# A decoder kernel: expert results added in the next block, an attention bias built later, a wait of the sorted experts moved back

## The reference, cut to what matters

```python
    # L2 ffn, second half: one of 8 experts per row
    idx = jnp.argmax(logits, axis=-1)
    mid = jax.nn.relu(jnp.einsum('th,ehf->etf', hn2, w1) + b1[:, None, :])
    y = jnp.einsum('etf,efh->eth', mid, w2) + b2[:, None, :]
    moe = y[idx, jnp.arange(hn2.shape[0])]
    ...
    x = x + _L3_attn_ref(_layernorm(x, axis=-1), ...)    # gated attention in groups of 64 rows
    x = x + _L3_xattn_ref(_layernorm(x, axis=-1), ctx_1024, ctx_1024, fside_BxS2_0, ...)
    x = x + _L3_ffn_ref(_layernorm(x, axis=-1), ...)     # two of 8 experts per row
    ...
    # in _L3_xattn_ref: the bias that is added to the scores
    ct = jnp.cumsum(session_deltas, axis=1)
    pairwise_delta = jnp.abs(ct[:, :, None] - ct[:, None, :])
    scores = scores + (time_bias_weight * jnp.log1p(pairwise_delta))[:, None, :, :]
```

## Time and profile before

| what | us |
|---|---|
| runs | 2972.42, 2975.32, 2977.95; median 2975.32 |
| the profiled execution | 2969.33 |
| its span in the trace | 2967.4 |

### The profile page before, as it was taken

One profiled execution on the slowest core, in us unless ns is written; L12 is line 12 of the kernel. 1 busy time (PEld: TensorE's weight loads), 2 busy tenths in 40 slices (PEclk: granted clock), 3 DMA queues, 4 the chain that ended last, 5 costly groups with the idle time before them and its releaser, 6 DMA issues. The chain is left out here.

```text
span 2967.4 us, 47859 instructions
## 1 busy us (share of the span) xinstructions
PE 2559.4 (86%) x16117; PEld 1874.6 (63%) x16117; DVE 1810.5 (61%) x4091; ACT 1313.7 (44%) x3205; POOL 808.7 (27%) x627
## 2 busy tenths in 40 slices
PE   4998989999688785999998989959969687869997
PEld 2666756666455453777676767649945465448886
DVE  7866976589788544344455559953355688444443
ACT  2334654266778234434343436623332565323332
POOL 5533520054000332222221216621110243132222
PEclk8999999999888798999999999979989898989999
DMA  9001000000200423000001010051120300531110
GB/s 321 2 1 49 14 19 1 15 1 1 65 4 1 109 87 125 29 1 1 1 1 50 12 42 31 2 206 37 37 76 1 90 12 1 182 118 49 51 49 26
DMA packets 152050, 142.43 MB, mean 48 GB/s; under 512 B 59948, under 2 KB 136770, under 8 KB 151428
## 3 DMA queue, kind: packets, MB, share of 16 engines
q1 hardware_dynamic: 139668, 110.61, 12.6%
q0 software_dynamic: 10560, 27.19, 2.7%
q10 hardware_dynamic: 1584, 1.57, 0.2%
HBM read 98.14 MB, written 43.02 MB: 48 GB/s over the span
## 5 line engine op out<-in xcount | busy, mean ns | idle before, releaser
L953 POOL TENSOR_TENSOR room<-room 128x1024 f32<-128x1024 f32 x144 | 273.1, 1896 | 464.0 <-DVE room L888 463.7
L882 DVE TENSOR_REDUCE room<-room 128x8 f32<-128x1024 f32 x144 | 174.1, 1209 | 0.0
L1420 PE MATMUL l3f_out<-room,Y 128*128 x624 | 141.0, 379 | 0.0
L953 POOL TENSOR_TENSOR room<-room,Y 128x1024 f32<-128x1024 f32 x32 | 60.7, 1896 | 252.0 <-DVE Y L888 252.0
L1420 PEld LDWEIGHTS l3f_out<-room,Y 128*128 128x128 f32 x624 | 115.6, 190 | 14.2
L1025 ACT ACTIVATE room<-l2a_scores,Y 128x128 f32<-128x128 f32 x256 | 71.9, 380 | 86.7 <-DVE Y L874 86.7
L609 PE MATMUL l2a_proj<-room 128*128 128x256 f32 x384 | 97.5, 398 | 11.6 <-ACT room L977 11.6
L2461 POOL DMA_INDIRECT sorted_rows<-room,l1f_place_i x32 | 31.0, 968 | 267.1 <-DVE l1f_place_i L2172 257.7
L1025 ACT ACTIVATE room<-l3x_scores,room 128x128 f32<-128x128 f32 x256 | 73.3, 401 | 55.3 <-DVE room L874 55.3
L1025 ACT ACTIVATE room<-l1a_scores,room 128x128 f32<-128x128 f32 x256 | 71.4, 386 | 58.6 <-DVE room L874 58.6
L1025 ACT ACTIVATE room<-l0x_scores,room 128x128 f32<-128x128 f32 x256 | 70.5, 384 | 59.4 <-DVE room L874 59.4
(11 more groups left out here) (838 smaller groups left out, 6909.3 us busy)
## 6 DMA issues: line engine op xcount, KB each, us to landing
sorted_rows<-head SPq DMA_DIRECT2D x1, 16640.0 KB, 57.0
room<-in_L_ffn_w SPq DMA_DIRECT2D x16, 1024.0 KB, 13.0
room<-in_L_ffn_W SPq DMA_DIRECT2D x16, 1024.0 KB, 12.0
Y<-sorted_rows SPq DMA_DIRECT2D x62, 130.0 KB, 2.1
room<-in_ctx SPq DMA_DIRECT2D x24, 256.0 KB, 2.9
room<-sorted_rows SPq DMA_DIRECT2D x39, 130.0 KB, 2.1
room<-results SPq DMA_DIRECT2D x8, 512.0 KB, 7.1
room<-in_L_ffn_routed_w SPq DMA_DIRECT2D x4, 512.0 KB
```

The lines of the kernel that those rows point to most:

```text
L882: dve.tensor_reduce(rsum[:, u % 2, :], p[:, u % (TURN + 1), :, :], AX.X, ALU.add)
L953: pool.tensor_tensor(p[:, u % (TURN + 1), :, :], p[:, u % (TURN + 1), :, :], rinv[:, u % (TURN + 1), :].unsqueeze(2).to_broadcast([P, HEAD ...
L1420: mm = pe.matmul(obank[n % 2][:, 0:D], hT[:, n % 2, f, :], chip.room[:, bass.ds(at + (SLOT // 2 + f * D), D)], start=(f == 0), stop=(f == ...
```

## The change

Three edits stand in the diff.

1. `l2fm` ends with the first group: SP fetches one piece, VectorE adds it and makes its statistics. The gated attention fetches the other three pieces into `pend` at its start. VectorE's `combine(g)` adds one group and makes its four statistics, one group in each of slots -2, -1 and 0; in slot 0 follow the roots of the 12 tiles and the second group's normalisation, which stood in slot -2.
2. `l3x`: the running-sum matmul and its copies move behind the opening's projections; the weighting is done for four tiles ahead of the slots and for the other twelve in slots 1 to 3.
3. `l3f`: `dest` gets four columns, and `aim(n)` waits for the scatter of tile n-4 instead of n-2.

```diff
@@ attention_block, tensor
-                if plan.mask == "timebias":
-                    pe.wait_ge(raw_loaded[0], 32)
-                    pe.matmul(out[:, 0:NB], chip.upper[:, :], deltas[:, :], start=True, stop=True).then_inc(ct_ready, 1)
...
-                for f in opening + bias_turns:
+                for f in opening:
+                    project((0, f))
+                if plan.mask == "timebias":
+                    pe.wait_ge(raw_loaded[0], 32)
+                    pe.matmul(out[:, 0:NB], chip.upper[:, :], deltas[:, :], start=True, stop=True).then_inc(ct_ready, 1)
+                for f in bias_turns:
                     project((0, f))
@@ attention_block, vector (the copies move likewise, behind the opening)
+                def biased(n):
+                    dve.wait_ge(log_ready, n + 1)
+                    dve.scalar_tensor_tensor(out=bias[:, n * 4:n * 4 + 4, :], in0=gap[:, n * 4:n * 4 + 4, :], scalar=w.v["tb"],
+                                             in1=keywide[:, n * TG:(n + 1) * TG].rearrange("p (j k) -> p j k", j=4), op0=ALU.mult, op1=ALU.add)
+                    dve.drain()
+
                 if plan.mask == "timebias":
                     dve.wait_ge(key_ready, 1)
-                    for n in range(NB // 4):
...
+                    biased(0)
...
+                    if plan.mask == "timebias" and 1 <= t < NB // 4:
+                        biased(t)
@@ sorted_experts_block
+    DESTS = 4 if last else 2
...
-                    for g in range(NG):
-                        for c in range(keep):
-                            part = results[c * TOK:(c + 1) * TOK, :].rearrange("(s b) d -> s b d", b=NB)[:, g * GR:(g + 1) * GR, :]
-                            sp.dma_start(back[c][:, g * GR:(g + 1) * GR, :], part).then_inc(gathered[g], 16)
+                    part = results[0:TOK, :].rearrange("(s b) d -> s b d", b=NB)[:, 0:GR, :]
+                    sp.dma_start(chip.Y[:, 0:GR, :], part).then_inc(gathered, 16)
                     prefetch.load(sp)
...
-                    if n >= 2:
+                    if last and n >= 4:
+                        dve.wait_ge(returned[par], (n // 2 - 1) * 16)
+                    if not last and n >= 2:
                         dve.wait_ge(returned[par], n // 2 * 16)
@@ gau_block, sync
+                for g in range(1, NG):
+                    part = chip.results[0:NB * P, :].rearrange("(s b) d -> s b d", b=NB)[:, g * GR:(g + 1) * GR, :]
+                    sp.dma_start(pend[:, (g - 1) * GR:g * GR, :], part).then_inc(pend_loaded[g], 16)
                 if prefetch:
                     prefetch.load(sp)
@@ gau_block, vector
+                def combine(g):
+                    dve.wait_ge(pend_loaded[g], 16)
+                    those = slice(g * GR, (g + 1) * GR)
+                    dve.tensor_tensor(chip.X[:, those, :], chip.X[:, those, :], pend[:, (g - 1) * GR:g * GR, :], ALU.add)
+                    for b in range(g * GR, (g + 1) * GR):
+                        sums(b)
...
-                        if g + 1 < NG:
+                        if 0 < g < NG - 1:
                             normalise(g + 1)
+                    if k < 1:
+                        combine(k + 3)
+                    if k == 0:
+                        dve.drain()
+                        ln_stats_vector(chip, dve, chip.X, rest, have="mv", part=slice(GR, NB))
+                        normalise(1)
@@ gau_block, scalar
+                    if k == 0:
+                        ln_stats_scalar(chip, act, rest, part=slice(GR, NB))
+                        act.preload_act_table(ACT.Silu)
```

More of the change, by code:

```diff
@@ L852, in _ @@
                         empty((0, f))
+                if plan.mask == "timebias":
+                    dve.wait_ge(raw_loaded[0], 32)
+                    for n in range(NB // 4):
+                        dve.tensor_copy(dwide[:, n * 4:n * 4 + 4, :], deltas[:, n * 4:n * 4 + 4].unsqueeze(2).to_broadcast([P, 4, P])).then_inc(wide_ready, 1)
+                    dve.wait_ge(ct_ready, 1)
+                    dve.tensor_copy(ctcol[:, :], out[:, 0:NB])
+                    dve.drain()
                 if chip.has_head:
@@ L1200, in sorted_experts_block @@
         final_rows = chip.out.rearrange("b s d -> (b s) d")
-        back = [chip.Y, chip.room[:, 0:NB * D].rearrange("p (b d) -> p b d", b=NB)]
         first_turned = 1 if chip.has_head else 0
@@ L1236, in sorted_experts_block @@
         returned = [sem("returned0"), sem("returned1")]
-        gathered = [sem(f"gathered{g}") for g in range(NG)]
+        gathered = sem("gathered")
         combined, summed = sem("combined"), sem("summed")
@@ L1734, in _ @@
                     empty_out(n)
[L1736 to L1748, removed]
+                if not last:
+                    dve.wait_ge(gathered, 16)
+                    dve.tensor_tensor(chip.X[:, 0:GR, :], chip.X[:, 0:GR, :], chip.Y[:, 0:GR, :], ALU.add).then_inc(combined, 1)
                     dve.drain()
-                    for b in range(g * GR, g * GR + 2):
+                    for b in range(2):
                         dve.bn_stats(chip.bn[:, b, :], chip.X[:, b, :])
                     dve.drain()
-                    for b in range(g * GR, g * GR + 2):
+                    for b in range(2):
                         dve.bn_aggr(chip.mv[:, b, :], chip.bn[:, b, :])
+                    dve.wait_ge(summed, 1)
+                    dve.tensor_scalar(chip.mv[:, 2:GR, 1], chip.mv[:, 2:GR, 1], 1.0 / D, None, ALU.mult)
+                    dve.drain()
+                    ln_stats_vector(chip, dve, chip.X, final, have="mv", part=slice(0, GR))
                 dve.drain()
[L1756 to L1760, removed]
-                    ln_stats_vector(chip, dve, chip.X, final, have="mv")
             @block.scalar
@@ L1822, in _ @@
                     act.preload_act_table(ACT.Sqrt)
[L1823 to L1832 removed]
+                    act.wait_ge(combined, 1)
+                    for b in range(2, GR):
+                        act.activation(chip.Y[:, b, :], chip.X[:, b, :], ACT.Identity, scale=1.0 / D, accum_out=chip.mv[:, b, 0:1])
+                    act.drain()
+                    for b in range(2, GR):
+                        op = act.activation(chip.Y[:, b, :], chip.X[:, b, :], ACT.Square, bias=chip.mv[:, b, 0:1], scale=-1.0, accum_out=chip.mv[:, b, 1:2])
+                    op.then_inc(summed, 1)
+                    ln_stats_scalar(chip, act, final, part=slice(0, GR))
             @block.gpsimd
@@ L2563, in gau_block @@
         oT = sb("oT", [P, OC, P])
+        pend = sb("pend", [P, NB - GR, D])
+        pend_loaded = [sem(f"pend{g}_loaded") for g in range(NG)]
+        rest = {n: sem(f"rest_{n}") for n in ("var_ready", "std_ready")}
         bank = [chip.ps(f"gau_bank{i}", scope) for i in range(8)]
```

24 lines of the change are left out of this document (5 added, 19 removed).

## The result

The changed kernel takes 2964.26 us in the median of ten runs (2959.86 to 2969.99), the kernel before 2980.26 in ten runs beside them (2972.42 to 2987.71; the three of the table ahead are among them). The ratio is 0.995, with a 95% interval of 0.9937 to 0.9964: faster by 0.5%. The difference of the medians is 16.0 us; the forecast was 10.8 us and 2964.5 us.

The account below looks back on a forecast made before the run. In `l3f` the gather, addition and scatter ring and TensorE were both near the bound, the ring a little ahead. -4.6 + 8.6 + 2.4 - 7.5 - 9.7 = -10.8 us, from 2975.32 to 2964.5 us; range 2959 to 2970, widened to 2957 to 2975.

Parts of the forecast that it names:

- End of `l2fm`: End of `l2fm`: three issues leave SP's stream, SP reaches the barrier last, the next block starts at 2173.07; -4.6 us.
- Start of the gated attention: Gated attention's opening: the moved combines delay the third tile's projection, +8.6 us, and TensorE's clock adds +2.4.
- The walk to the second `bias_v`: Gated attention: VectorE's steps added up from the block's start; second `bias_v` ends at 25.6 us, 17.0 before.
- The clock term: Gated attention: TensorE, idle some 6 us, may then run at half clock; between nothing and half of 7 us, taken +2.4.
- 12.6 are put there: Gated attention, before the features L2704: VectorE has 3.7 us of idle time, and 12.6 us of work are put there.
- Cross attention: Opening of `l3x`: bias matmuls at 10.4 instead of 17.55 us, three weightings spread; -7.5 us (-6 to -8.2).
- `l3f`: Last block's loop: `aim` and SP's row load come 1.78 us earlier, TensorE's wait ends; -9.7 us, other end 0.
- The ring then needs 7.37 - 0.49 = 6.9 us per tile: `l3f`, addition to addition through scatter and gather: gather 0.49 us shorter without a load beside it; TensorE, some 7.25, becomes the bound.
- That the ring stays: Rival, chance 0.23: in `l3f` the gather stays slow, additions follow by 7.4 to 7.7 us; gain 0, total 2974.2 us.
- The gated attention hid less: Rival, chance 0.09, that the gated attention hides more: its +11.0 shrinks to +4, total 2957.5 us.
- GpSimd was not held: Rival, chance 0.06: in `l3f` `aim` holds GpSimd's scatter issue beyond 1.03 us; +12 in place of -9.7, total 2986 us.
- The bias did come earlier: Rival, chance 0.03: cross attention's first projections wait for something else, the 7.5 us go; 2972 us, no change.

Follow-up runs that it names:

- the spread kernel: The changed kernel with combines spread: group 1 in slot -2, groups 2 and 3 in slots 1 to 4; 2969.55 us against 2991.90, ratio 0.9922.
- the one-row kernel: The kernel before, but from tile 2 on SP's load in `l3f` brings one row instead of 128; one run, 2994.71 us beside 2990.58.

## Why the prediction was right, point by point

**The time and the sign held**, and the sum held because errors cancelled. By the means over the profiles of kernels that have an edit or lack it, the stages give -6.4, +13.9, -10.3 and -12.0 us: -14.8, where the medians give -16.0 and I forecast -10.8. That the time came out within 0.3 us of the forecast is luck in part: the kernel before was 5 us slower in the ten runs beside the change than in the three of the table ahead.

**End of `l2fm`, forecast -4.6, measured -6.3.** SP is the last to the barrier, as said. The sum was mis-sized in one term: I took the remaining issues at their old lengths, and they became 1.7 us shorter in all, with less in the queue ahead of them (an argument; it wasn't tried alone).

**Start of the gated attention, forecast +8.6 and +2.4, measured +13.9** (149.8 and 147.9 us in the two profiles with this opening, 134.9 before). The walk to the second `bias_v` was right to 0.3 us, but for the product beside GpSimd: it gave 25.6, the trace has 27.25, and with GpSimd moved away 25.9. So the rule that I had left out of the sum, that of the Trainium skill (SBUF — State Buffer, section on the two separate sides), holds here: 2.29 us instead of 0.69. The clock term was a little small: the block grew by 4.7 us beyond the 10.2 (2.8 in the other profile). The granted clock was 0.50 for 6.8 us behind `bias_v` in both, 3.4 us at most, and in this one for 3.4 us more at the block's end, 1.7 at most; together that covers both numbers, an estimate from the rows of the clock. That this cost is one of place, "12.6 are put there", the spread kernel confirmed.

**Cross attention, forecast -7.5, measured -5.6 in the pair, -10.3 in the means.** The opening is as walked: 10.4 us to the bias matmuls, to the tenth, and 21.3 to the exponentials (forecast about 22). What failed is the block behind it, which I took as fixed but for 0.7 us: from the first exponential on it took 198.5 to 205.8 us in six executions of the same code, with the granted clock of the block between 0.89 and 0.92.

**`l3f`, forecast -9.7, measured -12.0 in the means** (424.2 us in four profiles without the edit, 412.2 in five with it). The size was nearly right by luck, the mechanism mostly wrong. Right: the load moves ahead of the gather and TensorE's waits go. Wrong: "The ring then needs 7.37 - 0.49 = 6.9 us per tile". Both terms failed. The 7.37 is one tile; the mean is 7.72 before and 7.42 after, 0.30 less. The 0.49 is half of 3.13 - 2.15, two gathers of the earlier trace rows that move no rows at all, and the load isn't what sets them apart either. Beside the longer one start two 8 KB fetches, 1.59 and 1.73 us after its issue (0.00 MB on queue 0, where a full tile has 0.13). The same gather is as long in the one-row kernel, again with two such fetches and without the load's traffic:

```profile
2958.06 3.17 DMA Y<-out,l3f_dest
...
2965.57 2.15 DMA Y<-out,l3f_dest
```

A full gather needs 2.79 with no load at all. Of the ring's 12.3 us (295.2 in the mean of the four profiles, 282.9 in the five) the 16 KB fetches gave 7.4, the 8 KB ones 1.7 and the load's place about 2; the rest lies in the tiles of padding. Wrong with it: "TensorE is the bound". The ring is, at 7.45 us per tile in the median.

**The rivals.** That the ring stays was half true: by its own sign, additions that follow by 7.4 to 7.7 us, it holds (7.42), and the gathers near 2.4 us did not come (2.78 in the median); but the ring was longer than that before, got shorter all the same, and its 2974.2 us did not come. TensorE's 98% came true and proved nothing. The gated attention hid less, not more. GpSimd was not held: the scatter's issue takes 1.00 us still. The bias did come earlier.

## What to carry to other kernels

Work that is moved behind a barrier isn't hidden by it: look for the slot whose engine really waits, since the same combines cost 14 us in the first three slots and 5 when spread. A change of several joined edits should be run edit by edit; here one of three was a loss of 7 us under a total that looked like success. Before a short transfer among the last tiles is taken for what a transfer costs without its neighbour, check that it moves the same bytes. And in a ring of dependent transfers read the distribution, not one tile: more than half of what was won here lay in a dozen long ones.

What beats both kernels is the change without its first edit, 0.9910. Spread combines, GpSimd behind the squares and four columns together were not run; by their stages they would lie some 4 us below it, an estimate (hand-over 10.0 for 16.1 us, `gau` 137.1 for 134.9); the 1.5 us that the same sum gave for the spread combines didn't show in their ratio.

## What the hardware showed that I had not expected

An indirect gather or scatter of 128 rows is 1.08 us longer in the mean, and up to 2.02, when a single 16 KB instruction fetch, about 1 us long, starts 0.8 to 2.0 us after its issue, among the transfer's data; with a fetch that starts before that it is 0.08 longer. In a loop that is bound by such transfers this made 8 to 12 us, and with the fetches at other places in the ring about 7 less.

TensorE read as 99.5% busy in a loop whose every tile waited for a DMA: a busy share near one did not show it to be the bound.

A VectorE product of two SBUF operands took 2.29 us beside a GpSimd addition and 0.69 without it.

The same code in `l3x` took between 218.7 and 227.1 us in six executions, with the granted clock between 0.89 and 0.92.
